# Moving the second low half of every rotated unit from VectorE to POOL, in a two-layer attention and expert kernel

## The reference, cut to what matters

```python
xn = _rmsnorm(x, gamma1)
q = (xn @ q_w + q_b).reshape(b, s, H, HD).transpose(0, 2, 1, 3)
k = (xn @ k_w + k_b).reshape(b, s, H, HD).transpose(0, 2, 1, 3)
v = (xn @ v_w + v_b).reshape(b, s, H, HD).transpose(0, 2, 1, 3)
...
x1, x2 = (x[..., 0::2], x[..., 1::2])
return jnp.concatenate([x1 * cos - x2 * sin, x1 * sin + x2 * cos], axis=-1)
```

## Time and profile before

| | |
|---|---|
| median of 3 runs | 1285.86 us (1280.12 to 1287.24) |
| profiled execution | 1287.74 us, its span 1286.0 us |
| busy over the span | PE 1035.9, DVE 747.3, POOL 634.2, ACT 559.5 us |
| second projection's loops | from about 318 to 528 us of the span |

### The profile page before, as it was taken

How to read it: one execution, slowest core, us unless ns; L and a number is a source line. 1 busy time by engine, 2 the same in 40 slices (tenths; PEclk the granted TensorE clock), 3 DMA queues, 4 the chain that set the end, 5 groups by cost and what they waited for, 6 DMA issues and landing times. The chain is left out here.

```text
span 1286.0 us, 23342 instructions
## 1 busy us (share of the span) xinstructions
PE 1035.9 (81%) x5894; PEld 736.7 (57%) x5895; DVE 747.3 (58%) x2002; ACT 559.5 (44%) x1143; POOL 634.2 (49%) x965
## 2 busy tenths in 40 slices
PE   4858899973988889399999999966798179999741
PEld 2435555542755657276666666634675159999610
DVE  7656566657888989665656566501442763333344
ACT  1226688862243343266666666610222005555400
POOL 5002333344654645276666666644451156666376
PEclk9898899985989979599999999988898559999955
DMA  5775644442566647767767667448671804455544
GB/s 159 261 261 152 175 127 126 124 143 85 192 224 239 241 172 285 235 176 207 215 196 212 184 183 211 146 135 221 182 215 36 253 22 134 134 133 129 101 132 117
DMA packets 172540, 221.02 MB, mean 172 GB/s; under 512 B 25410, under 2 KB 106081, under 8 KB 172482
## 3 DMA queue, kind: packets, MB, share of 16 engines
q1 hardware_dynamic: 160722, 196.69, 49.6%
q0 software_dynamic: 6048, 16.52, 6.1%
q10 hardware_dynamic: 5712, 7.13, 1.9%
HBM read 129.86 MB, written 90.28 MB: 171 GB/s over the span
## 5 line engine op out<-in xcount | busy, mean ns | idle before, releaser
L768 DVE CUSTOM_DVE_ANT_0 a_junk<-a_sc,keep_mask_qk 128x512 bf16<-128x512 f32 (+3 forms) x512 | 231.5, 489 | 188.5 <-PE a_sc L607 177.3
L572 POOL TENSOR_SCALAR_AFFINE_SELECT a_probs<-a_probs 128x128 f32<-128x128 f32 (+1 forms) x384 | 124.1, 330 | 290.7 <-ACT a_probs L728 290.6
L728 ACT ACTIVATE a_probs<-a_st 128x512 f32<-128x512 f32 (+1 forms) x384 | 196.1, 526 | 95.2 <-PE a_st L616 91.6
L623 PE MATMUL a_ob<-a_probs,a_vals 128*32 128x512 f32 (+7 forms) x1024 | 143.9, 454 | 3.8 <-POOL a_probs L572 2.4
L1094 POOL TENSOR_TENSOR rope_rot<-rope_wqkv 128x512 f32<-128x512 f32 x64 | 93.6, 1478 | 106.4 <-DVE rope_wqkv L1166 106.3
L1719 POOL DMA_INDIRECT ex_xg<-an,ex_idc x78 | 79.2, 1015 | 59.0 <-POOL ex_idc L1716 40.7
L606 PE MATMUL a_sc<-a_ka,a_qa 128*128 128x512 f32 (+3 forms) x256 | 87.2, 351 | 21.8 <-DVE a_ka L776 19.9
L1391 PE MATMUL mx_op<-keep_ow,mx_oT 128*128 128x256 f32 x256 | 68.6, 427 | 34.0 <-POOL mx_oT L1411 32.6
L1791 DVE COPY ex_w<-keep_w 128x514 f32 x78 | 33.6, 431 | 96.0 <-ACT ex_hid L1775 93.6
L616 PE MATMUL a_st<-a_qm,a_km 128*128 128x512 f32 (+3 forms) x256 | 85.3, 335 | 0.0
L590 POOL TENSOR_TENSOR a_part<-a_part,a_probs 128x256 f32<-128x256 f32 (+1 forms) x128 | 79.6, 622 | 10.0
(11 more groups left out here) (256 smaller groups left out, 2226.9 us busy)
## 6 DMA issues: line engine op xcount, KB each, us to landing
a_qa<-qs SPq DMA_DIRECT2D x128, 128.0 KB, 3.7
ks<-rope_rot SPq DMA_DIRECT2D x56, 256.0 KB, 2.5
qs<-rope_rot SPq DMA_DIRECT2D x56, 256.0 KB, 2.5
keep_w<-in_L_ffn_re_w SPq DMA_DIRECT2D x54, 256.0 KB, 5.0
o<-a_osb SPq DMA_DIRECT2D x48, 256.0 KB, 2.7
ye<-ex_y SPq DMA_DIRECT2D x78, 128.0 KB
qs<-rope_roth SPq DMA_DIRECT2D x32, 256.0 KB, 2.5
vs<-rope_vout SPq DMA_DIRECT2D x16, 512.0 KB, 3.3
```

What stands on the lines that cost most here:

```text
L572: return pool.affine_select(out=cols, in_=cols, compare_op=ALU.is_ge, fill=0.0, base=0, pattern=[[0, cols.shape[1]], [1, P]], channel_mult ...
L623: mm = pe.matmul(ob[M * hh:M * hh + M, P * kb:S], vals[:, n % 2, kb, hq, :], probs[:, (4 * n + hq) % 8, KCOL[kb]:KCOL[kb] + KLEN[kb]], sta ...
L728: act.activation(probs[:, h % 8, lo:hi], st[:, lo:hi], ACT.Exp).then_inc(exp_done, 1)
L768: return dve.tensor_tensor_reduce(out=junk[:, JUNK[qb]:JUNK[qb] + n], in0=src, in1=c.mask_qk[:, S - n:S], scale=1.0, scalar=-3e38, op0=ALU ...
```

## The change

The subtraction that makes a low half becomes one function for both engines. VectorE calls it for half 0 of each unit at the old place in its queue, POOL for half 1, behind its rotation of the following unit and ahead of its side work. `rot_low`, the semaphore that releases the stores of low halves, becomes one for each half, since two engines now count. The order of the stores is as before.

```diff
-        rot_high, rot_low = a.sem("rot_high"), a.sem("rot_low")
+        rot_high, rot_low = a.sem("rot_high"), [a.sem(f"rot_low{i}") for i in range(2)]
...
+        def rotated_low(eng, u, half):
+            eng.wait_ge(rot_high, 2 * u + half + 1)
+            eng.tensor_tensor(rot[:, u % ROT, half, :].bitcast(F32R), rot[:, u % ROT, half, :],
+                              roth[:, u % ROT, half, :].bitcast(F32), ALU.subtract).then_inc(rot_low[half], 1)
...
-                for part, (done, src) in enumerate(((rot_high, roth), (rot_low, rot))):
-                    for half in range(2):
-                        sp.wait_ge(done, 2 * u + half + 1)
-                        sp.dma_start(dst[part, half], src[:, u % ROT, half, :].bitcast(F32))\
-                          .then_inc(u_out[u % ROT], 16)
+                for half in range(2):
+                    sp.wait_ge(rot_high, 2 * u + half + 1)
+                    sp.dma_start(dst[0, half], roth[:, u % ROT, half, :].bitcast(F32)).then_inc(u_out[u % ROT], 16)
+                for half in range(2):
+                    sp.wait_ge(rot_low[half], u + 1)
+                    sp.dma_start(dst[1, half], rot[:, u % ROT, half, :]).then_inc(u_out[u % ROT], 16)
...
                     unit(UNITS * b + n)
+                    if b + n:
+                        rotated_low(pool, UNITS * b + n - 1, 1)
                     if b + 1 < B:
                         aside(b + 1, n)
+            rotated_low(pool, UNITS * B - 1, 1)
...
-            def rotated_low(u):
-                for half in range(2):
-                    dve.wait_ge(rot_high, 2 * u + half + 1)
-                    dve.tensor_sub(rot[:, u % ROT, half, :].bitcast(F32R), rot[:, u % ROT, half, :],
-                                   roth[:, u % ROT, half, :].bitcast(F32)).then_inc(rot_low, 1)
...
-                        rotated_low(UNITS * b + n - 1)
+                        rotated_low(dve, UNITS * b + n - 1, 0)
...
-            rotated_low(UNITS * B - 1)
+            rotated_low(dve, UNITS * B - 1, 0)
```

## The result

The changed kernel takes 1266.24 us (median of four runs, 1264.41 to 1267.23), the kernel before 1285.73 beside it: ratio 0.9855, 95% interval 0.9822 to 0.9887. Repeated twice with more runs it was 1268.27 (0.9879, 0.9854 to 0.9904) and 1268.35 (0.9886, 0.9860 to 0.9912), with before at 1283.73 and, over 23 runs, 1282.53. So the change brings between 14.2 and 19.5 us, and most likely about 14, which is what the larger samples say; the forecast was 8.2.

A forecast was written before the change was run, and what follows sets the result against it. VectorE was taken as the bound, with PE 0.20 us a unit behind in batch 3. Gains of 3.2 us in batch 0, 4.7 in batches 1 and 2 and 0.3 in batch 3 made 8.2, so 1278 us, range 1268 to 1285.

The forecast's parts named there:

- 1→2, the scalings of oT later: Start of batches 1 and 2: POOL's longer queue delays the scalings PE's output matmuls wait for, losing 0.85 us each.
- 2→3: Unit 2's products to unit 3's: VectorE is full, so removing its second subtraction gains 1.7 us a batch.
- 3→4, with L1145 blocked: Unit 3 to unit 4: 1.7 us saved, but a scalar operation waits for POOL's new subtraction, leaving 0.9.
- 4→6, with L826, L828, L1153 blocked: Unit 4 to unit 6: small VectorE instructions wait for POOL, losing 0.5 us up to the shift and 0.4 behind it.
- 6→7 and 7→0: Unit 6's products to PE's unit 0 of the next batch: gain 1.5 us a batch, nothing credited beyond.
- batch 3, products: Batch 3, without side work: PE-bound at 4.80 us a unit, VectorE's last products end about 1.5 us sooner.
- end of the stage: Tail behind the last products: POOL's last subtraction releases a store later, leaving 0.3 us of batch 3's 1.5 gain.
- PE then ends this stretch, at 4.8. Gain 1.5: Unit 6's products to PE's next unit 0: VectorE's way shrinks from 6.31 to 4.6 us, PE's turn and values set 4.8.
- Rival 2: Engines share rather than lock, or never meet: each step keeps its gain, 16 to 22 us, 1265 to 1271; chance 0.15.
- Rival 3: POOL's queue at a batch's start is later by the whole 2.56 us: gain only 3.9, 1282 us; chance 0.29.
- Rival 4: POOL's rotation waits for stores of the unit four earlier, with low halves leaving later: slower, 1302 us; chance 0.05.
- Rival 5: POOL's dearer subtraction falls on the path one for one: 19 us slower, 1307 us; chance 0.03.

The follow-up runs named there:

- after_third: The changed kernel run once more with no edit, beside three other kernels on the same chip: 1268.35 us, ratio 0.9886 to the kernel before.
- no_second_low: The changed kernel with the subtraction of half 1 left out on either engine, rotated values stored instead: 1249.93 us, ratio 0.9742 to the kernel before.
- before_again: The kernel before, run once more with no edit for another trace: 1280.98 us (one run).
- after_again: The changed kernel run once more with no edit: 1268.27 us, ratio 0.9879 to the kernel before.
- all_pool: The changed kernel with both low-half subtractions on POOL, none on VectorE: 1277.7 us, ratio 0.9960 to the kernel before.

## Why the prediction was wrong

**The base.** The sum was made against the profiled execution and then 1285.86. With 23 runs, before is at 1282.53. That is 3.3 us of the miss, and the output stage, which varied by 7 us between two traces, is one likely place. The prediction's 8.2 off 1282.5 would give 1274.3. From 1277.7 to the 1268.35 of after_third are 9.4 us: 3.3 of the base and 5.8 of the stage, worked out below, leave 0.3. The 1266.24 of the first four runs is 2.1 lower still.

**The sum, term by term** (measured: mean of the traces, batches 0 / 1 / 2):

| term | forecast | measured |
|---|---|---|
| 0→1 | 0 | 0.0 / 0.2 / 0.2 |
| 1→2, the scalings of oT later | 0 / -0.85 / -0.85 | 0.0 / -0.2 / -1.4 |
| 2→3 | 1.7 | 1.7 / 1.7 / 1.7 |
| 3→4, with L1145 blocked | 0.9 | 1.1 / 1.1 / 1.1 |
| 4→6, with L826, L828, L1153 blocked | -0.9 | -0.7 / -0.7 / -0.7 |
| 6→7 and 7→0 | 1.5 | 2.2 / 2.4 / 3.4 |
| batch 3, products | 1.5 | 1.7 |
| end of the stage | -1.2 | -0.8 |
| together | 8.2 | 14.0 |

The places and the mechanism were right. L1145, L826 and L828 were blocked as written, and L1153 (L1144 in before) as held possible; the shift comes at 402.49, 6.2 us behind unit 4 (forecast 6.5), and the steps 2→3 to 5→6 are each within 0.3 us of the forecast; what is left of it adds up to 1.2 us over three batches, 0.2 a batch at L1145, which waited 0.55 us and not 0.73, and 0.2 from unit 4 to unit 6 (0.3 less up to the shift, 0.1 more behind it).

**The step that failed** is "PE then ends this stretch, at 4.8. Gain 1.5". It followed the stretch from unit 6's products to the start of PE's unit 0 and stopped there, and gave the step from there into the next batch's products nothing. PE's timeline in after, end of batch 1, answers to the earlier trace rows:

```profile
412.49 1.15 PE L1031 MATMUL p_op<-keep_ident,p_xn 128*128 128x128 f32 x8 [3.11 <-DVE p_xn L1159]
...
417.01 0.75 PE L1046 MATMUL p_ub<-p_xh,rope_qm 128*128 128x512 f32 x1
417.56 0.63 PE L1046 MATMUL p_ub<-p_xlo,rope_qm 128*128 128x512 f32 x1
...
420.41 0.39 PE L1046 MATMUL p_ub<-p_xh,rope_km 128*128 128x512 f32 x1
```

and VectorE's:

```profile
416.84 0.74 DVE L1175 SCALAR_TENSOR_TENSOR rope_wqkv<-p_ub,rope_bqk,rope_cos 128x512 f32<-128x512 f32 x1
...
419.48 0.73 DVE L887 TENSOR_TENSOR rope_rot<-rope_rot,rope_roth 128x512 fp32r<-128x512 f32 x1
421.54 0.75 DVE L1175 SCALAR_TENSOR_TENSOR rope_wqkv<-p_ub,rope_bqk,rope_cos_q 128x512 f32<-128x512 f32 x1 [1.33 <-PE p_ub L1046]
```

The turn and the values take 4.52 us (412.49 to 417.01), nearly the forecast 4.64, and PE no longer waits 1.54 us for the low parts of xn. But the steps of VectorE are what counts. At this place it was full in before, up to the next batch's first products:

```profile
425.56 2.46 DVE L1173 TENSOR_TENSOR rope_rot<-rope_rot,rope_roth 128x512 fp32r<-128x512 f32 x2
427.93 0.74 DVE L1166 SCALAR_TENSOR_TENSOR rope_wqkv<-p_ub,rope_bqk,rope_cos_q 128x512 f32<-128x512 f32 x1
```
 Before, 6→7 was 6.17 with VectorE full; now it is 4.50, still with VectorE full, as its work has no PE in it but the turn that came in time: 1.7 gained, not 1.5. And 7→0 was full too in four of the six steps of before, 5.0 us with a pair of subtractions of 2.4; in the other two, of the first trace, VectorE also waited 0.37 and 0.61 us for PE (5.43 and 5.66). Now PE ends it, and VectorE waits 1.33. There I had no term, and it is worth 0.6, 0.7 and 1.7 us. How much hangs on PE's clock. Here the first matmuls of unit 0 run at half the clock; in the windows of the changed kernel (length; busy of PE, PEld, DVE, ACT, POOL; PEclk, DMA, GB/s):

```profile
416.00:420.00 4.00, 4.00 (x10) 2.85 (x10) 4.00 (x7) 1.36 (x3) 3.73 (x4) 0.50 0.46 167
420.00:424.00 4.00, 4.00 (x16) 2.81 (x16) 2.67 (x5) 1.46 (x3) 3.51 (x3) 0.97 0.57 209
```

0.50 is 1.2 GHz of 2.4. The matmuls of 0.63 us there are 0.39 at 2.4 GHz, and the step is 4.70. In the step from batch 2 to 3 of the same trace the clock rose with the start of the unit, as its second matmul shows, and the step is 3.45:

```profile
468.08 0.40 PE L1046 MATMUL p_ub<-p_xlo,rope_qm 128*128 128x512 f32 x1
```

In no_second_low, at the full clock, it is 3.30 to 3.31. Of the nine such steps in the three traces of after, five took 4.54 to 4.72 us, three 3.30 to 3.45 and one 4.15. So the part of this step's gain beyond about 0.3 us (5.00 to 4.70) depends on when the clock rises; the means of 0.6, 0.7 and 1.7 hold that chance, and what sets it stays open. I had weighed the low clock only for the values, and held it for the loss of a rival. Of the 5.8 us missed in the stage, 3.5 belong to this stretch (8.0 against 4.5), 1.2 to the blocked steps, 0.5 to 0→1 and 1→2, 0.6 to batch 3 and the end.

**The other terms.** The wait for the scalings of oT was put at 0.85 us a batch; it is 1.0 in the first traces of each (8.65 to 9.65 and 8.61 to 9.65), and 1→2 scatters by more: 10.30 in before_again, 10.82 in after_again. In before_again's window PE's clock was 0.85 to 0.87, in after_again's it was full, so the clock is not all of it; what the rest is stays open. Batch 3 went as written: steps of 4.80, VectorE waiting for PE.

**The rivals.** Rival 2 has the time that came (1265 to 1271), by a mechanism that the rows refute: no step kept its whole gain where a POOL instruction met one of VectorE's side work, and there were four such meetings a batch, three with a subtraction (L1145, L828, L1153) and one with a rotation (L826). Two slips in the rivals' prices: rival 2's parts add up to 5.5 a batch, not 5.4, and its 1265 to 1271 and rival 5's 1307 are counted from 1287.74, not from the median of 1285.86. Rival 3 needed 2.56 us at each batch's start, and it was 1.0. Rival 4, the ring of four: POOL's waits name VectorE and ScalarE, no store. Rival 5: POOL's whole new work costs 15.3 us against 29.3 of relief. The "Engine selection" section of the Trainium skill's GPSIMD Engine Reference advises against POOL for a two-input operation; the durations agree again (1284 against 752 ns, both medians), and still the time fell, for a stage is as long as its last wait, not as the sum of its engines.

## What to carry to other kernels

Where two engines lock each other out, price an instruction by what it blocks and is blocked by: the subtraction of 0.68 us cost VectorE 1.78 where POOL was at work, and moving it won 0.9 us a unit before POOL's own blocks took half back. Follow every step to the event that repeats (here VectorE's next products), not to an event on the way, and list each step that is full now, the one across a batch's end too. An order alone may bring nearly as much as another engine does: with both halves on VectorE, two units late, the stage gained 12.2 us where the change gained 14.1.

## What the runs showed of the hardware

- A VectorE instruction with one SBUF input and one scalar, on 128x4, is blocked as well (L1145 0.72 us and L1153 1.28 us, where 0.16 to 0.17 is free), while the bias and table products, with an input in PSUM, never are (731 to 753 ns in all fourteen traces).
- An untouched stage of one program varied between 109.9 and 117.2 us from one execution to the next; over all the kernels, whose output stage is the same, between 107.5 and 117.2. A single profile is no base for a sum of a few microseconds in another stage.
- An engine a little slower than the pace (POOL at 4.9 to 5.0 us a unit against 4.80, in all_pool) did not slow it over the seven steps of batch 3; it only fell behind, and the end then was 3.9 us longer.
- How long PE waited ahead of a turn of eight small matmuls went with the clock behind it: 0.33 to 0.74 us and 1.00 in the three turns of no_second_low, about 3 us and 0.50 in the nine of after. Where the low clock lasted through most of PE's next unit, the step from unit 7 to unit 0 took 4.54 to 4.72 us (five of the nine); where it ended as that unit began, 3.30 to 3.45 (three).
